# Second cross attention through A = Wq Wk^T: the context as keys and values, value weights after the mixing

## The reference

```python
q = jnp.einsum('bld,de->ble', query, Wq) + bq
k = jnp.einsum('bld,de->ble', key, Wk) + bk
v = jnp.einsum('bld,de->ble', value, Wv) + bv
scores = jnp.einsum('bqe,bke->bqk', q, k)
attn = jax.nn.softmax(scores, axis=-1)
out = jnp.einsum('bqk,bke->bqe', attn, v)
...
x = x + _L1_xattn_ref(_layernorm(x, axis=-1), ctx_512, ctx_512, L1_xattn_Wq, ...)
```

## Time and profile before

| | us |
|---|---|
| median of 3 runs | 1419.83 (1418.65 to 1424.13) |
| the profiled execution | 1422.47 |
| its span in the trace | 1420.7 |
| TensorE busy in it | 1295.5 (91%) |
| VectorE, ScalarE, GpSimd busy | 822.8, 668.3, 558.5 |
| granted TensorE clock, mean | 0.966 of 2.4 GHz |

### The profile page before, as it was taken

How to read it: one execution, slowest core, us unless ns; L and a number is a source line. 1 busy time by engine, 2 the same in 40 slices (tenths; PEclk the granted TensorE clock), 3 DMA queues, 4 the chain that set the end, 5 groups by cost and what they waited for, 6 DMA issues and landing times. The chain is left out here.

```text
span 1420.7 us, 30900 instructions
## 1 busy us (share of the span) xinstructions
PE 1295.5 (91%) x9938; PEld 1008.4 (71%) x9938; DVE 822.8 (58%) x1838; ACT 668.3 (47%) x1386; POOL 558.5 (39%) x763
## 2 busy tenths in 40 slices
PE   6999999989997675999788689999999999999998
PEld 5777777767775343777666457888888788888886
DVE  4666666656775885455688776444444444444443
ACT  4655555534453786554344353343343344343333
POOL 2233333346775333222577643333323232333332
PEclk9999999979999897999999899999999999999999
DMA  8100000000000000110000003333333253333331
GB/s 271 41 16 15 15 15 7 1 1 2 0 0 0 1 0 21 40 43 15 2 0 0 23 24 122 104 117 114 103 112 114 76 163 112 103 118 114 103 111 63
DMA packets 34038, 81.84 MB, mean 58 GB/s; under 512 B 4356, under 2 KB 11524, under 8 KB 33992
## 3 DMA queue, kind: packets, MB, share of 16 engines
q1 hardware_dynamic: 32952, 80.21, 17.5%
q10 hardware_dynamic: 1040, 1.05, 0.2%
HBM read 78.87 MB, written 2.38 MB: 57 GB/s over the span
## 5 line engine op out<-in xcount | busy, mean ns | idle before, releaser
L2096 POOL TENSOR_TENSOR sw<-sg,wb 128x512 f32<-128x512 f32 x136 | 176.6, 1299 | 398.4 <-ACT sg L1995 383.3
L2050 DVE TENSOR_TENSOR a<-sw,ps 128x512 f32<-128x512 f32 x136 | 93.6, 688 | 234.7 <-POOL sw L2096 234.6
L2000 ACT ACTIVATE ah<-a 128x512 fp32r<-128x512 f32 x136 | 86.0, 633 | 289.3 <-DVE a L2050 280.4
L1923 PE MATMUL ps<-Hh,wh 128*128 128x512 f32 x544 | 215.9, 397 | 3.2 <-DVE wl L2036 2.7
L1925 PE MATMUL ps<-Hh,wl 128*128 128x512 f32 x544 | 213.8, 393 | 0.0
L1924 PE MATMUL ps<-Hl,wh 128*128 128x512 f32 x544 | 213.0, 392 | 0.0
L626 ACT ACTIVATE Pr<-ps,mx 128x256 f32<-128x256 f32 x256 | 107.7, 496 | 116.7 <-DVE mx L528 116.5
L2054 DVE TENSOR_TENSOR al<-a,ah 128x512 fp32r<-128x512 f32 x136 | 94.2, 693 | 62.1 <-ACT ah L2000 58.6
L534 DVE COPY PT<-ps 128x512 f32<-128x512 f32 x128 | 88.4, 691 | 68.1 <-PE ps L393 68.1
L1923 PEld LDWEIGHTS ps<-Hh,wh 128*128 128x128 f32 x544 | 102.5, 188 | 26.0 <-issue 4.2
L1925 PEld LDWEIGHTS ps<-Hh,wl 128*128 128x128 f32 x544 | 102.7, 189 | 24.2
(11 more groups left out here) (219 smaller groups left out, 2671.6 us busy)
## 6 DMA issues: line engine op xcount, KB each, us to landing
wb<-token_weights SPq DMA_DIRECT2D x66, 512.0 KB, 3.6
raw<-in_ew SPq DMA_DIRECT2D x68, 384.0 KB, 3.1
cx<-in_ctxT SPq DMA_DIRECT2D x32, 256.0 KB, 2.7
X<-in_x SPq DMA_DIRECT2D x1, 1536.0 KB, 7.3
wqkv<-in_wqkv SPq DMA_DIRECT2D x2, 768.0 KB, 5.9
raw3g<-in_wg SPq DMA_DIRECT2D x1, 1024.0 KB, 5.4
raw3u<-in_wu SPq DMA_DIRECT2D x1, 1024.0 KB, 7.4
raw3d<-in_wd SPq DMA_DIRECT2D x1, 1024.0 KB, 9.6
```

Source lines behind the costliest of these rows:

```text
L1923: eng.matmul(ps[:, bank, :], wh[:, u, w], HhT[:, c, cols], start=(c == 0), stop=False)
L2000: eng.activation(ah[:, tt, :], a[:, tt, :], ACT.Copy).then_inc(m_ah, 1)
L2050: eng.tensor_tensor(a[:, tt, :], sw[:, tt, :], ps[:, UB[tt], :], ALU.mult).then_inc(m_a, 1)
L2096: eng.tensor_tensor(sw[:, tt, :], sg[:, tt, :], wb[:, u, tt * UT:(tt + 1) * UT], ALU.mult).then_inc(m_sw, 1)
```

## The change

It uses scores = (h Wq + bq)(ctx Wk + bk)^T = h A ctx^T + (Wk bq) ctx^T + a term of each query row alone, with A = Wq Wk^T (256x128). `setup` makes A on TensorE at the start of the stage, along with qb = Wk bq, kv = Wq bk and qk0 = bq bk. `qproj` now gives Q = h A + qb, 128 features, and the row's own term cq. `scores` multiplies Q with the context as it was loaded, cT, in plain float32. `keys` turns the context with four transposes, `keys_out` copies it to cN, `mix` multiplies it with the probabilities into U, and `vproj` multiplies U with Wv once per pair. The splits into high and low parts are gone, the keys, the values and their copies too. bv is added to X beforehand (`residual`, GpSimd). The number that Exp subtracts goes through two GpSimd subtractions (`offset`): cq - (cq - mx), where mx is the negated row maximum.

The pipeline gets deeper: body i works on pairs i-3 (X) to i+4 (statistics), the context has four buffers instead of two, and the loop has four bodies per turn, two turns, with the others unrolled. Names and line numbers in the rows of the new order are those of the changed file.

```diff
@@ -1373,253 +1373,301 @@
...
-    cx = sb("cx", [P, 2, 2 * CTX])
-    cxh = sb("cxh", [P, 2, 2 * CTX], F32R); cxl = sb("cxl", [P, 2, 2 * CTX], F32R)
-    wh = {n: sb(f"w{n}4h", [P, DIM], F32R) for n in "kv"}; wl = {n: sb(f"w{n}4l", [P, DIM], F32R) for n in "kv"}
-    QT = sb("QT4", [P, 2, HALF, P])
-    KT = sb("KT4", [P, 2, HALF, 2 * CTX])
-    V = sb("V4", [P, 2, 4, DIM])
+    R = 4
+    cT = sb("cT4", [P, R, 2 * CTX])
+    cN = sb("cN4", [P, 2, 4, CDIM])
+    wqT = sb("wqT4", [P, HALF, DIM]); wkT = sb("wkT4", [P, HALF, CDIM])
+    A = sb("A4", [P, HALF, CDIM])
...
+    SB, LB, QB, TB, UB, OB, CB = [0, 1], 2, 3, 4, 5, 6, 7
...
+    def pairs(eng, body):
+        for i in range(-3, 4):
+            body(i, i % R, i // R)
+        with eng.Fori(0, 2) as j:
+            for r in range(R):
+                body(R * j + R + r, r, j + 1)
+        for i in range(12, NPAIR + 3):
+            body(i, i % R, i // R)
...
-            def load(i, u):
-                sp.wait_ge(d_cxl, given(d_cxl) + i - 1)
-                sp.dma_start(cx[:, u, :], ctxT[:, i, :]).then_inc(d_ld[u], 16)
...
+            def load(i, r):
+                reach(sp, d_s, i - R + 1)
+                reach(sp, d_c, i - R + 1)
...
+            for i in range(NPAIR):
+                load(i, i % R)
...
+            def setup():
+                for c in range(HALF):
+                    for m in range(HALF):
+                        eng.transpose(ps[:, SB[1], (2 * c + m) * P:(2 * c + m + 1) * P], wq[:, m, c * P:(c + 1) * P],
+                                      ident[:, :])
+                for c in range(HALF):
+                    ins = eng.transpose(ps[:, TB, c * P:(c + 1) * P], wk[:, c * P:(c + 1) * P], ident[:, :])
+                ins.then_inc(d_set, 1)
+                eng.wait_ge(d_sev, 1)
+                for m in range(HALF):
+                    for c in range(HALF):
+                        eng.matmul(ps[:, SB[0], m * P:(m + 1) * P], wqT[:, c, m * P:(m + 1) * P], wkT[:, c, :],
+                                   start=(c == 0), stop=(c == 1))
+                for c in range(HALF):
+                    eng.matmul(ps[:, SB[0], 256:257], wkT[:, c, :], bqk[:, c:c + 1], start=(c == 0), stop=(c == 1))
+                for m in range(HALF):
+                    for c in range(HALF):
+                        eng.matmul(ps[:, SB[0], 257 + m:258 + m], wqT[:, c, m * P:(m + 1) * P], bqk[:, 2 + c:3 + c],
+                                   start=(c == 0), stop=(c == 1))
+                for c in range(HALF):
+                    ins = eng.matmul(ps[:, SB[0], 259:260], bqk[:, c:c + 1].to_broadcast([P, P]),
+                                     bqk[:, 2 + c:3 + c], start=(c == 0), stop=(c == 1))
+                ins.then_inc(d_set, 1)
...
-                for m in range(HALF):
-                    for c in range(2):
-                        ins = eng.matmul(ps[:, LQ, m * P:(m + 1) * P], wq[:, c, m * P:(m + 1) * P],
-                                         hT[:, u, c, :], start=(c == 0), stop=(c == 1))
+                for c in range(HALF):
+                    eng.matmul(ps[:, QB, 0:P], A[:, c, :], hT[:, u, c, :], start=(c == 0), stop=(c == 1))
+                for c in range(HALF):
+                    ins = eng.matmul(ps[:, QB, P:P + 1], hT[:, u, c, :], kv[:, c:c + 1],
+                                     start=(c == 0), stop=(c == 1))
...
                 for b in range(2):
-                    for c in range(HALF):
-                        ins = eng.matmul(ps[64 * b:64 * b + 64, SB[u], 0:CTX], QT[:, u, c, 64 * b:64 * b + 64],
-                                         KT[:, u, c, b * CTX:(b + 1) * CTX], start=(c == 0), stop=(c == 1),
-                                         tile_position=(0, 64 * b))
+                    ins = eng.matmul(ps[64 * b:64 * b + 64, SB[u], 0:CTX], Q[:, u, 64 * b:64 * b + 64],
+                                     cT[:, r, b * CTX:(b + 1) * CTX], start=True, stop=True,
+                                     tile_position=(0, 64 * b))
...
-            def pv(i, u):
-                eng.wait_ge(d_te, given(d_te) + i + 1)
-                eng.wait_ge(d_ve, given(d_ve) + 2 * i + 2)
-                eng.wait_ge(s_xdone, given(s_xdone) + base + i - 1)
+            def keys(i, r):
+                reach(eng, d_ce, i)
+                for t in range(4):
+                    ins = eng.transpose(ps[:, CB, t * P:(t + 1) * P], cT[:, r, t * P:(t + 1) * P], ident[:, :])
+                ins.then_inc(d_c, 1)
...
                 for b in range(2):
                     for kt in range(2):
-                        ins = eng.matmul(ps[64 * b:64 * b + 64, OB[u], 0:DIM], PT[:, u, kt, 64 * b:64 * b + 64],
-                                         V[:, u, 2 * b + kt, :], start=(kt == 0), stop=(kt == 1),
-                                         tile_position=(0, 64 * b))
...
+                        ins = eng.matmul(ps[:, UB, 64 * b:64 * b + 64], cN[:, u, 2 * b + kt, :],
+                                         PT[:, u, kt, 64 * b:64 * b + 64], start=(kt == 0), stop=(kt == 1))
+                ins.then_inc(d_u, 1)
+            def vproj(i, u):
+                eng.wait_ge(d_ue, i + 1)
+                reach(eng, s_xdone, given(s_xdone) + base + i)
+                eng.matmul(ps[:, OB, 0:DIM], UT[:, u, :], wv[:, :], start=True, stop=True).then_inc(d_o, 1)
...
+                if within(i, 0, last):
+                    scores(i, u, r, ld)
+                if within(i, 2, last + 2):
+                    mix(i - 2, u)
+                if within(i, -2, last - 2):
+                    normed(i + 2, u)
+                if within(i, -1, last - 1):
+                    qproj(i + 1, 1 - u)
+                if within(i, 0, last):
+                    keys(i, r)
+                if within(i, 1, last + 1):
+                    turn(i - 1, 1 - u)
+                if within(i, 2, last + 2):
+                    vproj(i - 2, u)
+            setup()
+            pairs(eng, body)
...
+            def keys_out(i, u):
+                eng.wait_ge(d_c, i + 1)
+                reach(eng, d_u, i - 1)
+                eng.tensor_copy(cN[:, u, :, :], ps[:, CB, :]).then_inc(d_ce, 1)
...
+            def body(i, r, ld):
+                u = r % 2
+                if within(i, 0, last):
                     rowmax(i, u)
-                if front and not opening(i):
-                    ln_dve2(eng, L, i + 1, v)
-                elif closing(i):
-                    ln_dve2(eng, L + 1, 0, v)
-                if isinstance(i, int) and i == NPAIR - 2:
+                if within(i, 1, last + 1):
+                    invert(i - 1, 1 - u, (r + 3) % R)
+                if within(i, 3, last + 3):
+                    add_x(i - 3, 1 - u, (r + 1) % R)
+                if within(i, -2, last - 3):
+                    ln_dve2(eng, L, i + 3, 1 - u)
...
+                if within(i, -3, last - 4):
+                    ln_dve(eng, L, i + 4, u)
...
+                if within(i, 0, last):
+                    keys_out(i, u)
...
-                    eng.activation(QT[:, u, m, :], ps[:, LQ, m * P:(m + 1) * P], ACT.Identity,
-                                   bias=bqk[:, m:m + 1]).then_inc(d_qe, 1)
...
+                eng.activation(Q[:, u, :], ps[:, QB, 0:P], ACT.Identity, bias=qb[:, :]).then_inc(d_qe, 1)
+                reach(eng, d_off, i - 1)
+                eng.activation(cq[:, u, :], ps[:, QB, P:P + 1], ACT.Identity, bias=qk0[:, :]).then_inc(d_qe, 1)
 
...
+            def mixed(i, u):
+                eng.wait_ge(d_u, i + 1)
+                reach(eng, d_o, i - 1)
+                eng.activation(UT[:, u, :], ps[:, UB, 0:P], ACT.Copy).then_inc(d_ue, 1)
...
+                if within(i, 2, last + 2):
+                    mixed(i - 2, u)
+                if within(i, -2, last - 2):
+                    reach(eng, d_q, i + 1)
+                    ln_act(eng, L, i + 2, u, LB)
+                if within(i, -1, last - 1):
+                    q_out(i + 1, 1 - u)
+                if within(i, 1, last + 1):
+                    turned(i - 1, 1 - u)
+                if within(i, 0, last):
                     exps(i, u)
...
-            def cx_low(i, u):
-                eng.wait_ge(d_cxh, i + 1)
-                eng.wait_ge(d_v, given(d_v) + 2 * i - 2)
-                eng.tensor_tensor(cxl[:, u, :], cx[:, u, :], cxh[:, u, :].bitcast(F32), ALU.subtract).then_inc(d_cxl, 1)
...
+            def offset(i, u):
+                eng.wait_ge(d_max, i + 1)
+                eng.wait_ge(d_qe, 2 * i + 2)
+                eng.tensor_tensor(top[:, u, :], cq[:, u, :], mx[:, u, :], ALU.subtract).then_inc(d_top, 1)
+                eng.wait_ge(d_top, i + 1)
+                reach(eng, d_exp, i - 1)
+                eng.tensor_tensor(off[:, u, :], cq[:, u, :], top[:, u, :], ALU.subtract).then_inc(d_off, 1)
+            def residual(i, u):
+                reach(eng, s_xdone, given(s_xdone) + base + i - 1)
+                eng.tensor_tensor(xb[:, u, :], X[:, i, :], bv[:, :], ALU.add).then_inc(d_xb, 1)
```

(54 more changed lines are left out.)

171 lines of the change are left out of this document (73 added, 98 removed).

## The result

| | before | after |
|---|---|---|
| median | 1420.06 (4 runs) | 1383.8 (1381.09 to 1386.86, 4 runs) |
| ratio of after to before, 95% interval | | 0.9736 [0.9708, 0.9765] |
| the profiled execution, its span | 1422.47, 1420.7 | 1385.44, 1383.6 |
| granted TensorE clock, mean | 0.966 | 0.961 |

The account below looks back on a forecast made before the run. The prediction took the stage as bound by TensorE's number of instructions. Scores(0) to scores(15) -39.0 us and drain +3.2 made -35.8, so 1384 on the median's scale, 1379 to 1389 by its own uncertainty; range with rivals 1377 to 1396.

Parts of the forecast that it names:

- first three pairs: Start of the stage's loop: bodies 0 and 1 lack mixing and value matmuls, 2.8 and 3.3 us; then 4.35 a pair.
- What bounds the kernel: In the changed stage, TensorE's instruction count sets the pace, 6.78 us a pair; work on other engines is hidden.
- rival 1: In the loop, another engine sets the pace: VectorE's strict order makes a pair 5.0 us, total 1392; 15%.
- The room of 0.2 to 0.5 us: In the loop, slack for ScalarE's copy of the turned context before TensorE's mixing in the next body needs it.
- The slots: TensorE's matmuls and transposes of one pair after the change, priced start to start: sum 3.54 us.
- The openings: In each pair after the change, seven TensorE groups begin behind a wait, 0.11 us each: 0.8 us.
- The clock: TensorE's granted clock in the changed stage: 1.00 from pair 1 on.
- Rival 2: TensorE's clock falls in part, to 0.8 for this stage: +0.9 us a pair, total 1396; 9%.
- The row against it: First cross attention, 2048 records of 17 columns that stream almost nothing, holds clock 1.00 for 238 us.
- Theory A: From the experiments, not the prediction: what TensorE streams brings full clock; one-column matmuls keep it busy without streaming.
- Rival 4: Half clock throughout the stage, short matmuls and waits leaving too little to stream: pair 7.9 us, total 1439; 3%.
- Setup and drain: Stage's ends: setup on TensorE leaves scores(0) at 572.8, bounds -2.3 and +0.9; drain 8.0 us, +3.2.

Follow-up runs that it names:

- e5_order: Kernel before, with TensorE's mixing and the second half of the value matmuls exchanged, so mixing stands directly ahead of the next scores; 1414.84 us, ratio 0.9946.
- e4_noterm: Changed kernel without the row's own term (kv, qk0, cq, the pairs' one-column matmuls and GpSimd's offset gone); 1371.47 us, ratio 0.9646.
- e1_wide: Changed kernel with the one-column matmuls of setup and every pair streaming 128 columns; 1377.26 us, ratio 0.9702.
- e2_fill: Changed kernel with eleven unread matmuls of 512 bf16 columns in the opening's waits; 1381.02 us, ratio 0.9718.
- e3_fillt: Changed kernel with 22 float32 transposes of 128 columns as fillers in the opening's waits; 1376.39 us, ratio 0.9699.
- e0_again: Changed kernel unaltered, run once more for a second trace; 1385.9 us, ratio 0.9761.
- e10_noterm2: Second look at the changed kernel without the row's own term; 1368.68 us in its single run.
- e7_lean: Changed kernel without the row's own term, setup's remaining one-column matmuls (qb) widened to 128 columns, no fillers; 1371.5 us, ratio 0.9669.
- e8_lean2: Second look at the same kernel as e7_lean; 1368.33 us, ratio 0.9646.
- e6_best: Changed kernel without the row's own term and with eleven unread 512-column bf16 matmuls in the opening's waits; 1365.45 us, ratio 0.9602.
- e9_best2: Second look at the same kernel as e6_best; 1365.91 us, ratio 0.9627.

## Why the prediction was right, and where it was wrong

| step | predicted | measured | error |
|---|---|---|---|
| scores(0) starts | 572.8 | 572.6 | -0.2 |
| first three pairs | 2.8 + 3.3 + 4.35 = 10.45 | 15.32 | +4.9 |
| twelve pairs more | 12 x 4.35 = 52.2 | 45.2 | -7.0 |
| last scores to the last X | 8.0 | 7.5 | -0.5 |
| later stages | as before | 1.6 longer | +1.6 |
| profiled execution | 1386.7 | 1385.4 | -1.3 |

**What bounds the kernel: right.** All of TensorE's removed time came off the end, no other engine is late, and rival 1 fell: the waits in the loop run to TensorE, none from it. VectorE, priced at 2.9 a pair, is busy 23.96 x 3.78 / 38 = 2.4. The room of 0.2 to 0.5 us between `turn` and `mix` was enough.

**The slots: right, one a little dear.** 3.54 were priced; with the one-column matmuls at the measured 0.37 for 0.45 it is 3.46.

**The openings: wrong, by 0.11 x 7.** "So 0.9 go to the starts of eight groups behind a wait, 0.11 each" was a division of a remainder by a count that fitted, not a reading. The pair before has two groups in 64-column tiles that stand apart, so four switches; e5_order takes two away and 0.33 goes. If the other two cost the same, that makes 0.66 of the 0.9 (0.60 by the single starts of before). The rest stays in e5_order too. The prediction saw it and spread it: "the first of a group takes 0.22 where the next take 0.117" is true of the values (603.04 to 603.26, 606.00 to 606.22) and, as 0.34 for 0.24, of the keys (601.16 to 601.50), the three groups on split operands. The inputs of the second values were ready 2.4 us before, so it isn't a late wait there. Each of the three follows float32 rows; whether that change of format is what costs the 0.10 was not tried. After has no split operands and no such first record. After has only one group in tiles, two switches, 0.33: 3.46 + 0.33 = 3.79, against 3.78 measured. The sum fits better than its parts: by the single starts the way into the scores costs 0.10 (0.53 for a slot of 0.43), the way out 0.16, and 0.07 stands at the mixing and the context's transposes. e4_noterm takes one group away and saves its slots alone. So the step counted the wrong events: it should have asked which groups open dear, and looked at their neighbours' shapes.

**The clock: wrong.** The prediction has full clock "from pair 1 on". It came with pair 3, in both traces of the kernel. The first three pairs at full clock take 9.0 to 9.2 (e1 to e3), so this costs 6.1 to 6.3 us there, and another 2 to 3 ahead of scores(0) (8.8 to 9.9 us of opening instead of 11.6, which the prediction had priced at half clock). Rival 2 named the clock, but as a partial fall all through the loop, taken from a stage with idle time; what happened was a half clock that lasted through 14.7 us without idle time, and full clock afterwards. The row against it, 1.00 over the first cross attention with its 17-column records, didn't carry over. It isn't that this stage never has to bring the clock up: ahead of the row's window, from 52.5 to 59.4 us, before is at half clock there too, and comes back within 6.8 us. But its 17-column records are only 68.4 of the 224.9 us of TensorE's busy time in that window, and between them run transposes and matmuls of 128 to 512 columns; "stream almost nothing" was a wrong reading of the stage. Rival 4's mechanism, too little to stream, is the one that the experiments bear out for the opening, and wrong for the loop. Why after's clock rises with pair 3 and then holds, with one-column matmuls in every pair, no run shows. Theory A holds in every trace (us from the stage's first matmul to full clock):

| kernel | one-column records and fillers | us |
|---|---|---|
| after, e0_again | one-column records in setup and pairs | 26.4, 29.4 |
| e4_noterm, e10_noterm2 | four one-column records left, in the setup | 13.7, 12.5 |
| e7_lean, e8_lean2 | none left | 5.8, 5.7 |
| e1_wide | all widened | 5.7 |
| e2_fill, e3_fillt | as after, fillers between | 3.9, 4.9 |
| e6_best, e9_best2 | as e4, fillers between | 5.3, 5.7 |

The last four lines can't be ranked among themselves: two traces of one kernel differ by up to 3 us.

**Setup and drain: right in size, the setup by a sum that doesn't add up.** The setup's terms make 11.0 us at half clock and some 7 at full, so from 561.4 they end at 572.4 and 568.5, and not at the 573.7 and 570.5 that the prediction gives; 572.8 was taken "as before". Measured are 11.65 us from a start at 560.95: 2.5 for the transposes and copies (2.3 priced), 5.1 for the 24 records (5.0), 1.6 to `qproj` (1.4), 2.4 to scores(0) (2.3). The later stages are the same work; their 1.6 us most likely go with the clock, which stands at its half level for 30 us in all behind this stage in after and for 25 in before. Such stretches move from run to run, and a forecast can't have them.

So the size of the gain was right by luck: with the openings right alone the forecast would have been 8 us lower, 1376 (7.0 in the loop, 1.2 in the first pairs), with the clock right alone some 6 higher, 1390.

## What to carry to other kernels

Price a group's opening by its neighbours: two groups in narrow tiles next to each other save two switches, and a remainder spread evenly over a count explains nothing until one of them is moved. A busy TensorE isn't a streaming one: matmuls of a single column cost nearly what 128 columns cost (0.09 and 0.11 a record), and the kernels that held more of them came to full clock later, so behind a quiet stretch widen them, fill the waits with matmuls that nobody reads, or drop the term; a term that is the same along the softmax needn't be computed at all. With the term gone and the waits filled the kernel takes 1365.5, 18 us less than after and 54 less than before; 16.0 of the 18 stand in the stage.

## What the runs showed of the hardware that I had not expected

- TensorE at half clock through 14.7 us (after) and 17.8 us (e0_again) without idle time, while float32 transposes, matmuls of 64 to 256 columns and one-column matmuls ran. In the kernel without the row term, widening the last four one-column records brings the full clock 7 to 8 us sooner (13.7 and 12.5 in e4_noterm and e10_noterm2, 5.8 and 5.7 in e7_lean and e8_lean2).
- 22 transposes in the waits of the opening bring the full clock 4.9 us behind its start, instead of 26.4 (e3_fillt).
- Passing between full-width matmuls and 64-column tiles costs 0.16 us each way, on average over the two that e5_order takes away.
- VectorE's h instruction (line 218) takes 0.41 in after's loop and took 0.77 to 0.86 in before's, where it ran beside GpSimd's subtraction of 1.28 us. That this pairing is the cause was not tried by itself, but e5_order speaks for it: the same h starts 0.2 us or more behind the end of that subtraction there (606.48 against 606.27) and takes 0.40 to 0.41 in each of its 14 rows.
